# A mamba, gated-MLP, attention and expert kernel over eight sequences: dt\*u products and half of the first pass's drive products on POOL, with new tile counts and new written orders

## The reference

```python
def mamba(x, Win, convw, convb, Wx, Wdt, bdt, Alog, Dp, Wout):   # 128 -> 256 channels, 16 states
    xi, z = split(x @ Win)
    xi = silu(causal_dwconv(xi, convw, convb))                   # 4 taps
    dt_in, B, C = split(xi @ Wx)                                 # 8, 16, 16 columns
    dt = softplus(dt_in @ Wdt + bdt)
    h[t] = exp(dt[t] * A) * h[t-1] + (dt[t] * xi[t]) * B[t]      # 256 channels x 16 states
    y[t] = sum_s h[t] * C[t] + xi[t] * Dp
    return (y * silu(z)) @ Wout
# block 1: one mamba forward, one on the reversed sequence, norms of both, a small feed-forward
# block 2: silu(x @ w1) * (x @ w2), gelu(@ h1), gelu(@ h2), @ w3
# block 3: causal attention, 8 heads, low-rank keys and values
# block 4: 8 experts of 256 hidden units, the two best of each token
```

## Time and profile before

| what | value |
|---|---|
| median of 3 runs | 1865.23 us (1862.81 to 1865.96) |
| the profiled execution | 1865.98 us, span 1864.2 us |
| TensorE busy | 1635.7 us (88%), mean granted clock 0.942 |
| VectorE busy | 1468.0 us (79%) |
| ACT busy | 1099.5 us (59%), of which 295.1 are 230 table loads |
| POOL busy | 750.1 us (40%) |
| DMA | 309.17 MB, mean 166 GB/s; q1 61.9% of 16 engines' span |

### The profile page before, as it was taken

One profiled execution on the slowest core, in us unless ns is written; L12 is line 12 of the kernel. 1 busy time (PEld: TensorE's weight loads), 2 busy tenths in 40 slices (PEclk: granted clock), 3 DMA queues, 4 the chain that ended last, 5 costly groups with the idle time before them and its releaser, 6 DMA issues. The chain is left out here.

```text
span 1864.2 us, 24264 instructions
## 1 busy us (share of the span) xinstructions
PE 1635.7 (88%) x8352; PEld 765.6 (41%) x8352; DVE 1468.0 (79%) x2032; ACT 1099.5 (59%) x1474; POOL 750.1 (40%) x601
## 2 busy tenths in 40 slices
PE   3454588999999999999998999899998998899888
PEld 1120134444444445443544445344544444444545
DVE  2999798789996999789997999799988998631514
ACT  3544486568745786569746785578746872452132
POOL 0555454435533453435533453435534453300102
PEclk7655699999998999999999999999999999999999
DMA  7999998678856794778766794779667794400000
GB/s 192 241 248 234 257 236 202 180 183 201 200 144 159 185 233 130 188 187 206 191 153 172 194 241 102 199 177 227 170 154 191 192 229 113 109 0 0 1 7 6
DMA packets 107886, 309.17 MB, mean 166 GB/s; under 512 B 15971, under 2 KB 32245, under 8 KB 107765
## 3 DMA queue, kind: packets, MB, share of 16 engines
q1 hardware_dynamic: 93556, 279.32, 61.9%
q10 hardware_dynamic: 14208, 28.32, 4.7%
HBM read 287.67 MB, written 19.92 MB: 165 GB/s over the span
## 5 line engine op out<-in xcount | busy, mean ns | idle before, releaser
L1531 POOL TENSOR_TENSOR sb_hc<-sb_hst,sb_crep 128x512 f32<-128x512 f32 x512 | 654.2, 1282 | 880.5 <-DVE sb_hst L1259 623.2
L1259 DVE TENSOR_TENSOR_SCAN sb_hst<-sb_ring,ps_in 128x512 f32<-128x512 f32 x512 | 620.1, 1211 | 20.9 <-ACT sb_ring L947 16.0
L947 ACT ACTIVATE sb_ring<-sb_ring,sb_A 128x512 f32<-128x512 f32 x512 | 345.8, 713 | 211.8 <-DMA sb_ring<-spread_dram 189.7
L1251 DVE TENSOR_TENSOR ps_in<-sb_ring,ps_brow 128x512 f32<-128x512 f32 x512 | 354.9, 693 | 30.6 <-DMA sb_ring<-spread_dram 18.3
L924 ACT ACT_TABLE_LOAD x230 | 295.1, 1283 | 13.6 <-DVE sb_xd L1310 3.2
L858 PE MATMUL ps_pair<-sb_mix,sb_ew 128*128 128x512 f32 x512 | 250.4, 623 | 6.6 <-DVE sb_g L1348 2.7
L637 PE MATMUL ps_y<-sb_hc,sb_const 128*32 128x512 f32 x1024 | 149.8, 659 | 64.3 <-POOL sb_hc L1531 54.7
L799 PE MATMUL ps_pair<-sb_g,sb_h 128*128 128x512 f32 x320 | 160.6, 625 | 21.9 <-ACT sb_mix L1105 15.4
L787 PE MATMUL ps_pair<-sb_h,sb_g 128*128 128x512 f32 (+3 forms) x512 | 164.4, 452 | 8.2 <-DVE sb_nmax L1400 4.3
L858 PEld LDWEIGHTS ps_pair<-sb_mix,sb_ew 128*128 128x128 f32 x512 | 94.1, 196 | 147.0 <-issue 103.1
L878 PEld LDWEIGHTS ps_pair<-sb_ew,sb_eh 128*128 128x128 f32 x1024 | 120.4, 192 | 21.3 <-issue 18.4
(11 more groups left out here) (208 smaller groups left out, 1890.7 us busy)
## 6 DMA issues: line engine op xcount, KB each, us to landing
sb_ring<-spread_dram SPq DMA_DIRECT2D x512, 512.0 KB, 6.0
spread_dram<-sb_dd ACTq DMA_DIRECT2D x32, 512.0 KB, 6.6
sb_brep<-cut_dram ACTq DMA_DIRECT2D x16, 256.0 KB, 7.4
sb_crep<-cut_dram ACTq DMA_DIRECT2D x16, 256.0 KB, 8.0
sb_xtok<-in_L_attn_x_dram SPq DMA_DIRECT2D x8, 256.0 KB, 4.8
sb_ew<-in_L_ffn_w_dram SPq DMA_DIRECT2D x2, 1024.0 KB, 12.3
out_dram<-sb_yy ACTq DMA_DIRECT2D x8, 256.0 KB, 5.1
sb_h<-in_L_ffn_h_w_dram SPq DMA_DIRECT2D x1, 1024.0 KB, 7.9
```

The lines of the kernel that those rows point to most:

```text
L947: act.activation(ring[:, n % RING, 0, :], ring[:, n % RING, 0, :], ACT.Exp, scale=A[d][:, g:g + 1]).then_inc(sem["dA"], 1)
L1251: dve.tensor_tensor(ps_in[n % 2][:], ring[:, n % RING, 1, :], ps_brow[:], ALU.mult).then_inc(sem["dbu"], 1)
L1259: dve.tensor_tensor_scan(hst[:, HST_SLOT[n], :], ring[:, n % RING, 0, :], ps_in[n % 2][:], 0.0, ALU.mult, ALU.add).then_inc(sem["scan"], 1)
L1531: pool.tensor_tensor(hc[:, n % 6, :], hst[:, HST_SLOT[n], :], crep[n // NU][:], ALU.mult).then_inc(sem["hc"], 1)
```

## The change

- **dt\*u to POOL.** All dt\*u products go from VectorE (`dt_step`) to POOL (`spreads`), which gets a stream h in its orders. The two of the first head run before pass 0.
- **Drives to POOL in pass 0.** Of the 64 units of pass 0 the odd ones (`BY_POOL`) have their drive made by POOL, in place in the ring's slot (`drives`, stream m). For these ACT writes exp(A dt) into the PSUM bank `ps_in[n % 2]`, and waits for scan n - 2 before. VectorE scans with the two operands changed about. A new semaphore `dbp` counts them.
- **Tiles.** `hst` 3 to 4, `hc` 6 to 8, `brep` and `xd` one for each direction; `wkd` and `rst4` share memory with other tiles to make room.
- **dt product over 128 rows.** `wdt` is zero and `xd` one outside the rows used.
- **Loads.** 13 of the 26 later loads are issued behind the first six ring loads of pass 0. The next sequence's x is asked for after the seventh ring load instead of the third.
- **Orders.** All strings are new, and pass 1, the final pass and the flush have strings of their own. In TensorE's body string the reduction of units 52 to 55 now stands between `ao` and its variance (the last two r), and two reductions, instead of one, stand between the first and the second turned scores (e0 and e1).

```diff
-    dA=64, dbu=64, scan=64, hc=64, yskip=4, gated=4, resid=2, sq=6, rstd=6, norm=6,
+    dA=64, dbu=64, dbp=32, scan=64, hc=64, yskip=4, gated=4, resid=2, sq=6, rstd=6, norm=6,
...
-RING, HST = 6, 3
-HST_SLOT = [n % HST for n in range(UNITS - 1)] + [1]
+RING, HST, HC = 6, 4, 8
+BY_POOL = range(1, UNITS, 2)
+HST_SLOT = [n % HST for n in range(UNITS)]
...
 ORDER = dict(
     PE=(
-        "xxxxxxuxrxxruxrxhrurhxrhruhxxrrrruhxrrhhurhruxrrruhxruxxrxxhxrxhxurrxhxrrrrrxrrrrrrrrrrrhruhhruhrhurrrruhrrrrr"
-        "urru"),
+        "xxxxxuxxrxxruxrxhrurhxrhruxrxrrrhhxrruxrrxuuhhrrrhruuhxrxxxrhxxhxurrxhrrrxrrrrrrrrrrrrrhrhhrhuurhurrrrrrrrruru"
+        "rxuh"),
     ACT=(
...
+        "muuummuumuumuuuummuuuuuhmummmuuumuuuumumumuumuumuuuummuumuhumuuumuuumuumuummuuuumumuuuumhmuumuuuhumu"))
...
+SECOND_ORDER = dict(
+    PE=(
+        "urrrhruhrruhrurhrrurrhrhrurhurrrrhhuurhrhrurrrrrhrrrrrrrrrrrrhrhhruhrhurrhrrrurrrrururu"),
...
-SECOND, _after = place(section(without(ORDER["PE"], "x")), later(_after))
+SECOND, _after = place(section(SECOND_ORDER["PE"]), later(_after))
...
-FINAL, _after = place(section(final(ORDER["PE"])), later(_after))
-FLUSH, _after = place(section(without(ORDER["PE"], "ugh")), later(_after))
+FINAL, _after = place(section(FINAL_ORDER["PE"]), later(_after))
+FLUSH, _after = place(section(FLUSH_ORDER["PE"]), later(_after))
...
-        wdt = sb("wdt", [64 + R + 2 * S + 1, DI])
+        wdt = [sb(f"wdt{d}", [P, DI]) for d in range(2)]
...
-        xd = sb("xd", [P, T])
-        brep = sb("brep", [P, T])
+        xd = [sb(f"xd{d}", [P, T]) for d in range(2)]
+        brep = [sb(f"brep{d}", [P, T]) for d in range(2)]
...
-        hc = sb("hc", [P, 6, T])
+        hc = sb("hc", [P, HC, T])
...
+        EARLY = 13
...
-                for dst, src in later:
+                for dst, src in later[:EARLY]:
...
+                    if n == RING - 1:
+                        with nc.allow_non_contiguous_dma(reason="per-channel vectors, once"):
+                            for dst, src in weights:
+                                sp.dma_start(dst, src).then_inc(w_later, 16)
...
-                    product(f"dtp{NH * d + h}", [wdt[rows, h * P:(h + 1) * P]], [xd[rows, :]])
+                    product(f"dtp{NH * d + h}", [wdt[d][:, h * P:(h + 1) * P]], [xd[d][:]])
...
+                dA = ring[:, n % RING, 0, :]
+                if n in by_pool:
+                    act.wait_ge(sem["scan"], row("scan", n - 1))
+                    dA = ps_in[n % 2][:]
+                act.activation(dA, ring[:, n % RING, 0, :], ACT.Exp, scale=A[d][:, g:g + 1]).then_inc(sem["dA"], 1)
...
+                        if pooled:
+                            act.wait_ge(sem["dbp"], pooled * (d + 1) + first("dbp"))
+                        act.dma_start(brep[d][:], cut[d, 0:S, :].unsqueeze(1).broadcast_to([S, CU, T])).then_inc(sem["brep"], 16)
...
-            def dt_step(row, hf):
-                d, h = divmod(hf, NH)
-                dve.wait_ge(sem["dt"], row("dt", hf + 1))
-                dve.tensor_tensor(dd[:, 1, :], dd[:, 0, :], u[d][:, h, :], ALU.mult).then_inc(sem["du"], 1)
...
+            def drive(row, n, step=1):
...
+            def scan(row, n, by_pool=()):
+                dA, dbu = ring[:, n % RING, 0, :], ps_in[n % 2][:]
+                if n in by_pool:
+                    dA, dbu = ps_in[n % 2][:], ring[:, n % RING, 1, :]
+                    dve.wait_ge(sem["dbp"], row("dbp", n // 2 + 1))
+                else:
+                    dve.wait_ge(sem["dbu"], row("dbu", n + 1))
...
-                dve.tensor_tensor_scan(hst[:, HST_SLOT[n], :], ring[:, n % RING, 0, :], ps_in[n % 2][:], 0.0,
-                                       ALU.mult, ALU.add).then_inc(sem["scan"], 1)
+                dve.tensor_tensor_scan(hst[:, HST_SLOT[n], :], dA, dbu, 0.0, ALU.mult, ALU.add).then_inc(sem["scan"], 1)
...
-                    drive(at(0), n)
-                    yield
+                    if n not in by_pool:
+                        drive(at(0), n, 2 if by_pool else 1)
+                        yield
...
-                pool.wait_ge(sem["y_red"], row("y_red", (n - 6) // 4 + 1 if n >= 6 else 0))
-                pool.tensor_tensor(hc[:, n % 6, :], hst[:, HST_SLOT[n], :], crep[n // NU][:], ALU.mult
+                pool.wait_ge(sem["y_red"], row("y_red", (n - HC) // 4 + 1))
+                pool.tensor_tensor(hc[:, n % HC, :], hst[:, HST_SLOT[n], :], crep[n // NU][:], ALU.mult
                                    ).then_inc(sem["hc"], 1)
+
+            def drives(at):
+                row = at(0)
+                for n in BY_POOL:
+                    pool.wait_ge(sem["brep"], row("brep", 16 * (n // NU + 1)))
+                    pool.wait_ge(sem[f"ring{n % RING}"], row(f"ring{n % RING}", 16 * (n // RING + 1)))
+                    pool.tensor_tensor(ring[:, n % RING, 1, :], ring[:, n % RING, 1, :], brep[n // NU][:], ALU.mult
+                                       ).then_inc(sem["dbp"], 1)
+                    yield
 
...
+            def spreads(row, d):
+                for hf in range(NH * d, NH * d + NH):
+                    pool.wait_ge(sem["dt"], row("dt", hf + 1))
+                    pool.tensor_tensor(dd[:, 1, :], dd[:, 0, :], u[d][:, hf % NH, :], ALU.mult).then_inc(sem["du"], 1)
+                    yield
+
+            def heads(at, nxt=True):
+                yield from spreads(at(0), 1)
+                if nxt:
+                    yield from spreads(at(1), 0)
...
+            alone(spreads(at(0), 0))
+            interleave(TURN_ORDER["POOL"], dict(h=heads(at), u=units(at, False), m=drives(at)))
```

More of the change, by code:

```diff
@@ L272 @@
+FLUSH_ORDER = dict(
+    PE=(
+        "xxxxxxxrxxrxrxrrxrrxrrrrxrrxxrrxrrrrxrxxrxxxrrrrxxrrrrrrrrrrxrrrrrrrrrrrrrrrxrrr"),
+    ACT=(
+        "xxxxxxxrrrxrxxxrxrrxrrrrrrrrxxrrrxrxxxxxrrrrrrrrrrrxrrxrrrrrrxrxrxrrxrrrrrrrrrrr"),
+    DVE=(
+        "xxxxxxrxxxrrxrxxrrrrrrxrrrrxxrxrxrxrrrxxxrxxrrrrxxrrrrrrrrrrrrrrrxrxrrrrrrrrrrrr"),
+    POOL=(
+        "rxrxrxxrrrxrrrrrrrrxrxxxxrrrxrrrxrrrrrrrxrrxrrxrrrrrxrrrrxxxxxxrrxrxrxrrrxrrrrxr"))
 NONE = {f"g{i}": None for i in range(4)}
@@ L1509, in _ @@
             at = counts(B - 1)
-            interleave(final(ORDER["DVE"]), dict(u=units(at, True), g=gates_of(at, True), r=rest(at, FINAL), x=experts(at, FINAL), h=heads(at, FINAL, False)))
+            interleave(FINAL_ORDER["DVE"], dict(u=units(at, True), g=gates_of(at, True), r=rest(at, FINAL), x=experts(at, FINAL), h=heads(at, FINAL, False)))
             at = counts(B)
@@ L1513, in _ @@
             gate(at, -1, 3, True)
-            interleave(without(ORDER["DVE"], "ugh"), dict(r=rest(at, FLUSH), x=experts(at, FLUSH)))
+            interleave(FLUSH_ORDER["DVE"], dict(r=rest(at, FLUSH), x=experts(at, FLUSH)))
             at = counts(B + 1)
@@ L1520, in _ @@
         def _(pool):
-            pool.memset(wdt[:], 0.0).then_inc(w_zero, 1)
-            pool.memset(xd[:], 1.0)
+            pool.memset(wdt[0][:], 0.0)
+            pool.memset(wdt[1][:], 0.0).then_inc(w_zero, 1)
+            for d in range(2):
+                pool.memset(xd[d][:], 1.0)
             pool.memset(nsplit[:], 0.0)
```

142 lines of the change are left out of this document (74 added, 68 removed).

## The result

The kernel after takes **1846.11 us**, the median of 6 runs (1841.71 to 1855.11), against 1865.6 us of the kernel before on the same chip (6 runs, 1862.81 to 1869.13). The ratio is 0.99, with a 95% interval of 0.9873 to 0.9927: 19.5 us faster. The forecast was 1831 (1804 to 1858). The profiled execution is the fastest of the six, 1841.71 us with a span of 1839.9, so that the two traces lie 24.3 us apart. A second trace of the same kernel, `after_again` (span 1838.3), shows how far two executions differ.

The account below looks back on a forecast made before the run. Pass 0 was taken as bound by DMA and nearly equally VectorE, pass 1 by nothing full, middle passes by TensorE. From 1865.98 us, -5 -4 -6 -10 -3 -4 -3 = -35 gave 1831 us, range 1804 to 1858.

Parts of the forecast that it names:

- Start, -5: Before the first decay: thirteen weight loads moved behind the sixth ring load let it start sooner; -5 us, bounds -6.3 and -2.
- The three us at VectorE's first turning step: At the start: VectorE's first turning step waits for the last of the thirteen late weight loads, perhaps 3 us.
- Pass 0, -4: Pass 0: VectorE loses drive and dt*u products, but the DMA bound stays; -4 us, near the low end.
- rival A: Pass 0: VectorE was the bound after all, so the term is -22 instead of -4, 1813 us; chance 0.20.
- Pass 1, -6: Pass 1: its own orders recover a fifth of 30.7 us idle time; -6 us, bounds -14 and +3.
- Middle, -10: Five middle passes: shorter TensorE waits and a cheaper dt product give -2.0 us a pass, -10 for five.
- Both waits that the change touches: Middle passes, TensorE: 1.51 us before the attention variance and 2.27 us before the second scores, each shortened by 1.0 us.
- the other two ... keep what stands ahead of them: Middle passes, TensorE: waits before the attention product and before the next pass's first step keep what stands ahead of them.
- Clock, -3: Middle passes: shorter waits may keep the clock at its upper level; -3 us, up to -7.
- Final and flush, -7: Final pass and flush: own orders and more tiles give -4 and -3 us; bounds -8 and +3 for both.
- Rival B: Middle passes do not gain, since any order only shifts chains of dependent steps about; 1847 us, chance 0.16.
- Rival C: POOL's dt*u products queue behind read-outs and delay spread and ring loads, making the kernel slower, 1887 us; chance 0.08.

Follow-up runs that it names:

- loads_first: Kernel after with all 26 later weight loads again issued ahead of the first ring load: 1849.93 us, ratio 0.9904.
- dve_drives: Kernel after with the odd units' drive products of pass 0 back on VectorE, dt*u staying on POOL: 1846.46 us, ratio 0.9885.
- ends_filtered: Kernel after with final pass and flush run by the body's new strings with letters left out, instead of their own orders: 1846.16 us, ratio 0.9886.
- norm_psum: Kernel after with the reciprocal root of a pass's last two normalizations written to the variance's PSUM bank: 1834.96 us, ratio 0.9823.
- b_tiles: Kernel before with only the change's deeper tiles (HST = 4, HC = 8), its own orders kept: 1856.8 us, ratio 0.9951.

## Why the forecast was right, and where it was not

- **The whole.** 1846.11 lies in the range and faster was right, but the likeliest case's own range (1818 to 1843) missed it, and so did the point, by 15 us. Trace against trace 10.7 us are missing (9.1 in the second trace); the rest is that the profiled execution is faster than the median.
- **Start, -5.** Right in size: -6.4 at the first decay. The three us at VectorE's first turning step are 7.2, and `loads_first` shows 4.2 of 5.4 us given back in pass 0.
- **Pass 0, -4.** That the loads are a bound was right, rival A fell. `dve_drives` gives up to 3.7 us for the drives, but in the sum with the late weights the stage gained nothing: the two terms together were -9 and came to -6.1.
- **Pass 1, -6.** -7.1 and -6.1 in the two traces, but -4.3 in `ends_filtered`, which has the same two passes. The term was a fifth of the idle time, taken without a wait behind it, and it is near by luck: of the 5.7 us between the windows 3.8 are TensorE's busy time (160.52 and 156.76 for the same 828 matmuls), 1.9 its idle time. (Half of 30.7 is 15, not the 14 of its bound.)
- **Middle, -10.** Right in size, in part for other reasons. The traces give -6.2 and -11.6, and with the clock taken out -9.6 and -9.8. The forecast had 1.4 us less idle time a pass (two waits of 1.0, less 0.6 for the copy of xd) and 0.6 less for the dt product. TensorE's idle time fell by only 0.6 us a pass (46.2 to 43.3 and 42.9 in five). Both waits that the change touches shrank as forecast, and the copy of xd costs 0.5. What failed is "the other two ... keep what stands ahead of them": it looked at the steps ahead on TensorE alone. The wait at the next pass's first step grew from 1.23 to between 2.17 and 2.4, because the burst on POOL held up VectorE's product, and a wait of 0.7 for VectorE's `sb_eh` (L684) is new as well and gone in `norm_psum`. With the hold-up taken out, `norm_psum` has 7.7 us of idle time in a middle pass, on average, against 9.2 before: -1.5, about the forecast's -1.4. The -2.27 us wait was credited to the reduction moved; its cause was misread as a table load, and the deeper tiles alone take 1.4 us of it in each pass. What made the sum come out is TensorE's busy time, 1.5 us less a pass at full clock (195.70 and 194.24). The dt product gives 0.4 of it; the rest is small differences over many groups of matmuls, and its cause is open.
- **Clock, -3.** The forecast asked for 1.00 in all middle passes. They have 0.98 or 0.99 in the first trace, and one of five has 1.00 in the second; before it was three of five. From the first boundary on, before has 45.1 us at the lower level, after 44.9 and 38.0: nothing gained, or some 3.5 us. Nearly all of the 6.8 us by which the first trace missed the forecast in the middle is this term (3.4 us lost, by the estimate, where 3 were to be won). In `norm_psum`, whose waits at the boundary are shorter, it is 27.8.
- **Final and flush, -7.** -5.1 and -3.1, for another reason. The flush was to lose its 4.9 us wait; with stages cut at the boundaries that wait stands at the end of the final pass, in both kernels, and is 3.9 after, and the flush became longer. The final pass gained 8.2, of which 5.8 are TensorE's busy time (192.63 and 186.83, 1020 matmuls), for the most part the clock: 10.3 us at 0.50 before, none after. That is in part luck of the execution profiled, since other traces with the same final pass have 200.3 to 206.3 us. `b_tiles` shows 208.5 to 203.8 for the tiles alone.
- **Rival B** (1847: the middle does not gain) is nearest in time, but not in its mechanism: the middle did gain, and what hid a part of it was the clock and a new wait that no chain of the order alone opened. **Rival C** did not come. One dt\*u product in each middle pass does start 7.1 us behind its softplus, as rival C had it, but on VectorE before it was 6.6, and VectorE waits for ring loads 2.2 us in the five middle passes together, 4.6 before. In passes 0 and 1 one product starts 33.2 and 20.7 us late; what that costs there no run parts.

## What to carry to other kernels

When work moves to POOL or is bunched there, look through VectorE's instructions that stand beside it for those with two SBUF operands, or with an operand and per-partition scalars in SBUF, first of all those that TensorE waits for; putting one operand in PSUM took away the hold-up and gave 10 us, some 4 of them at equal clock. Before two kernels are compared by a stage, take the time at the lower clock out of both: here it hid 3.5 us of the change's gain in one trace and added 1.7 in another. Deeper tiles change when a busy engine works, not only how far it runs ahead, and so should be measured alone before orders are written around them. Half the bytes took some 7 us off a stage whose loads filled the DMA engines: before work is moved off an engine, try what the stage takes without its supposed bound.

The fastest version measured that computes the whole is `norm_psum`, 1834.96 us, 1.8% below the kernel before and 10 us below the kernel after.
